# One exponential per wavelength, stacked sums, and a new order of VectorE's work in a multi-wavelength attention block

## The reference

```
for w in range(16):
    scores = einsum('bhqd,bhkd->bhqk', Q*m[w], K*m[w]) * SCALE      # m = cos(pm)
    scores = scores * cos(KERR * scores * scores)                    # KERR = 2.7e-12
    acc += softmax(scores) @ V * iw[w]
attn = (acc / 16) @ Wo + bo
x = layernorm(x + attn)
```

## Time and profile before

| what | value |
|---|---|
| three timed runs | 7163.84, 7164.55, 7164.82 us; median 7164.55 |
| the profiled execution's own time | 7165.78 us |
| its span, first to last instruction | 7164.2 us |
| TensorE's mean granted clock | 0.944 of full |
| ScalarE busy | 6960.6 us, 97% |
| TensorE busy | 5953.2 us, 83% |
| VectorE busy | 5710.1 us, 80% |

### The profile page before, as it was taken

How to read it: one execution, slowest core, us unless ns; L and a number is a source line. 1 busy time by engine, 2 the same in 40 slices (tenths; PEclk the granted TensorE clock), 3 DMA queues, 4 the chain that set the end, 5 groups by cost and what they waited for, 6 DMA issues and landing times.

```text
span 7164.2 us, 125922 instructions
## 1 busy us (share of the span) xinstructions
PE 5953.2 (83%) x46020; PEld 2131.5 (30%) x46020; DVE 5710.1 (80%) x7952; ACT 6960.6 (97%) x2227; POOL 116.6 (2%) x244
## 2 busy tenths in 40 slices
PE   7877878887888888888888888888888888888877
PEld 2222222222323233233233233233232332332335
DVE  6777877777888888888888888888888888888873
ACT  6999999999999999999999999999999999999992
POOL 0000000000000000000000000000000000000000
PEclk8999999999999999999999999999999999999998
DMA  2000000000001001001000010010010010010001
GB/s 61 2 4 4 4 2 4 4 2 17 23 21 29 17 27 29 18 25 32 20 27 29 15 29 23 22 29 23 24 32 17 27 29 16 27 29 18 27 19 36
DMA packets 61133, 151.59 MB, mean 21 GB/s; under 512 B 10272, under 2 KB 28576, under 8 KB 60320
## 3 DMA queue, kind: packets, MB, share of 16 engines
q1 hardware_dynamic: 55648, 140.04, 6.8%
q10 hardware_dynamic: 4160, 2.10, 0.1%
q0 software_dynamic: 768, 1.57, 0.1%
HBM read 132.66 MB, written 11.01 MB: 20 GB/s over the span
## 4 chain that ended last, share of the span: by engine, by line
ACT 56%; issue 25%; PE 10%; ACTq 7%; DVE 2%; DMA 0%; SPq 0%; DVEq 0%
ACT ring L592 55%; PE pv L661 6%; ACTq L587 5%; ACTq L588 1%; DVE scores L797 1%; PE sc L1120 1%; PE pv L668 1%; PE tr L1128 1%; PE sc L644 1%; ACT L606 0%; ACTq L580 0%; PE sc L625 0%; DVE rowmax L787 0%; PE sc L278 0%; ACTq L157 0%
## 5 line engine op out<-in xcount | busy, mean ns | idle before, releaser
L592 ACT ACTIVATE ring<-scores 128x4096 f32<-128x4096 f32 (+3 forms) x2048 | 6752.9, 3391 | 27.1 <-DVE scores L797 20.4
L661 PE MATMUL pv<-ring,vh 128*32 128x512 f32 x30720 | 4022.8, 638 | 1130.3 <-ACT ring L592 1123.0
L661 PEld LDWEIGHTS pv<-ring,vh 128*32 128x32 f32 x30720 | 1009.1, 115 | 3809.5 <-issue 2109.5
L829 DVE COPY numer<-pv 128x512 f32<-128x512 f32 x512 | 352.4, 688 | 481.6 <-PE pv L668 477.2
L797 DVE COPY scores<-sc 128x1024 f32<-128x1024 f32 (+1 forms) x512 | 601.9, 1217 | 75.7 <-PE sc L644 72.7
L823 DVE SCALAR_TENSOR_TENSOR vprobs<-ring,vprobs 128x1024 f32<-128x1024 f32 x512 | 627.2, 1225 | 19.1 <-issue 1.5
L822 DVE SCALAR_TENSOR_TENSOR vprobs<-vprobs,vbits 128x1024 f32<-128x1024 f32 x512 | 627.2, 1225 | 17.5
L787 DVE TENSOR_REDUCE rowmax<-sc 128x1 f32<-128x1024 f32 x512 | 601.4, 1216 | 40.2 <-PE sc L625 39.0
L821 DVE SCALAR_TENSOR_TENSOR vprobs<-ring 128x1024 f32<-128x1024 f32 x512 | 622.6, 1216 | 2.9
L668 PE MATMUL pv<-vpower,vlast 128*32 128x512 f32 x2048 | 532.1, 595 | 0.0
L668 PE MATMUL pv<-vprobs,vlast 128*32 128x512 f32 x2048 | 529.6, 592 | 0.0
(11 more groups left out here) (157 smaller groups left out, 2655.8 us busy)
## 6 DMA issues: line engine op xcount, KB each, us to landing
tile_w<-in_L_ffn_w SPq DMA_DIRECT2D x192, 512.0 KB, 4.0
qt<-q_scratch SPq DMA_DIRECT2D x256, 36.0 KB
kt_<-k_scratch SPq DMA_DIRECT2D x256, 36.0 KB
ring<-in_L_ffn_w SPq DMA_DIRECT2D x2, 2048.0 KB, 12.6
ring<-in_L_attn_x ACTq DMA_DIRECT2D x4, 512.0 KB, 7.4
q_scratch<-ring SPq DMA_DIRECT2D x4, 512.0 KB, 4.8
k_scratch<-ring SPq DMA_DIRECT2D x4, 512.0 KB, 5.6
v_scratch<-ring SPq DMA_DIRECT2D x4, 512.0 KB, 5.2
```

The lines of the kernel that those rows point to most:

```text
L592: nc.scalar.activation(ring[:, i % SLOTS, 0:cols], scores[:, bass.ds(n % 2, 1), half * CK:(half + 1) * CK, :].rearrange("p o k s -> p (o k ...
L661: last = nc.tensor.matmul(sums, vh[:, buf, half * CK + k, :], ring[:, 2 * half + w2, col:col + HALF], start=(half == 0 and k == 0), stop=( ...
```

## The change

- `ring` becomes 2 slots of 8192 columns. ScalarE makes all key tiles of a wavelength in one instruction, of 8192 columns for even wavelengths and 7168 for odd ones; the 1024 columns left out are VectorE's as before. It waits for the whole of the head's scores before the first, and loads its register before each.
- `weigh_values` takes one wavelength per step. The four column groups are now 2 query halves x 2 halves of the keys. Up to three wavelengths share a PSUM bank: the values stand in `vh` with zeros on both sides (`VW` columns), and a window of 32 columns moves by 9 for each of them, so that each adds into rows of its own. A bank is full after wavelengths 2, 5, 8, 11, 13 and 15 (`FILLS`).
- `copy_numer` copies one bank per fill, six per head in place of eight. `transpose_numer` is now four matmuls against a 64-column `fold` matrix, which add the two key halves and transpose at once; it runs behind the weighing in steps 3, 6, 9, 12 and 14, and the last one behind the weighing of step 0 of the next head. `normalise` runs three times per head in place of four (steps 6 and 12, and step 1 of the next head, followed there by `sum_wavelengths`).
- In `vector_head` the exponential work comes ahead of the maxima, the copies of scores and the tile's pieces of its step; `exponents` moves to odd steps and `polynomials` to even ones, for a pair that is used one step later than before. `exponents` gets a wait for the weighing that last read its `vpower` buffer.
- The tile's small matmuls of part 1 write to a bank of their own (`tr[:, 1]`) at separate columns and wait for `tile_logits_made` of the tile before instead of the normalisation; `tile_slice` 0 waits for `tile_x1T_made`.
- `layer_norm` takes three Newton steps in place of four.

The diff, cut to its core; of loops and functions that are rewritten only the new side is shown:

```diff
 G = 4
 QG = S // G
-NCH = 2 * W
 CK = KT // 2
-SLOTS = 4
+SLOTS = 2
+CHUNK = (KT * S, (KT - 1) * S)
+VR = D + 1
+STACK = 3
+VW = VC + (STACK - 1) * VR
+VAT = (STACK - 1) * VR
+FILLS = ((0, 1, 2), (3, 4, 5), (6, 7, 8), (9, 10, 11), (12, 13), (14, 15))
+NF = len(FILLS)
+FILL_OF = [f for f, ws in enumerate(FILLS) for _ in ws]
+GROUPED = [(f, f + 1) for f in range(0, NF, 2)]
 GT = 4
 NG = B * S // (GT * P)
...
-        ring = sb("ring", [P, SLOTS, CK * S])
-        vh = sb("vh", [P, 2, KT, VC])
+        ring = sb("ring", [P, SLOTS, KT * S])
+        vh = sb("vh", [P, 2, KT, VW])
-        vmant = ring[:, SLOTS - 1, (CK - 1) * S:CK * S]
-        vlast = sb("vlast", [P, 2, 2, VC])
+        vmant = ring[:, 1, CHUNK[1]:KT * S]
+        vlast = sb("vlast", [P, 2, 2, VW])
-        numer = sb("numer", [P, 2, HALF])
-        parts = sb("parts", [P, W // 2, 8, 2, D])
+        numer = sb("numer", [P, HALF])
+        parts = sb("parts", [P, 2 * KT, D, W // 2])
+        fold = sb("fold", [P, 2 * VC])
...
             then(nc.vector.tensor_scalar(y_.bitcast(I32), var_.bitcast(I32), -0.5, RSQRT_SEED, ALU.mult, ALU.add))
-            for _ in range(4):
+            for _ in range(3):
                 then(nc.vector.tensor_tensor(t_, y_, y_, ALU.mult))
                 then(nc.vector.scalar_tensor_tensor(t_, t_, -0.5, var_, ALU.mult, ALU.mult))
                 then(nc.vector.scalar_tensor_tensor(y_, t_, 1.5, y_, ALU.add, ALU.mult))
...
             def quads(n, first, last):
                 with act.Fori(first, last) as quad:
-                    for i in range(8):
-                        pair, half, w2 = i // 4, (i // 2) % 2, i % 2
-                        w, chunk = 4 * quad + 2 * pair + w2, NCH * n + 8 * quad + i
-                        if i in (0, 2):
-                            act.wait_ge(sc_free, USES * n + ROW_USE + 1 + CK * (half + 1))
-                        if half == 0:
-                            act.reg_load(scale[w2], scale_bits[:, bass.ds(w * H + n % H, 1)])
+                    for i in range(4):
+                        w, chunk = 4 * quad + i, W * n + 4 * quad + i
+                        if i == 0:
+                            act.wait_ge(sc_free, USES * (n + 1))
+                        act.reg_load(scale[i % 2], scale_bits[:, bass.ds(w * H + n % H, 1)])
                         act.wait_ge(slot_free, chunk + 1)
                         apart(act)
-
-                        cols = CK * S - (S if half == 1 and w2 == 1 else 0)
-                        nc.scalar.activation(ring[:, i % SLOTS, 0:cols],
-                                             scores[:, bass.ds(n % 2, 1), half * CK:(half + 1) * CK, :].rearrange("p o k s -> p (o k s)")[:, 0:cols],
-                                             ACT.Exp, scale=scale[w2]).then_inc(probs_ready, 1)
+                        nc.scalar.activation(ring[:, i % SLOTS, 0:CHUNK[i % 2]],
+                                             scores[:, bass.ds(n % 2, 1), :, :].rearrange("p o k s -> p (o k s)")[:, 0:CHUNK[i % 2]],
...
+        def weigh_values(pe, n, buf, w):
+
+
+            f = FILL_OF[w]
+            j, pair, w2 = FILLS[f].index(w), w // 2, w % 2
+            first, final = j == 0, w == FILLS[f][-1]
+            window = slice(VAT - j * VR, VAT - j * VR + VC)
+            if w == 0:
                 pe.wait_ge(vh_ready, n + 1)
+            pe.wait_ge(probs_ready, W * n + w + 1 + START)
             for k in range(CK):
                 for g in range(G):
+                    qh, kh = g // 2, g % 2
+                    kt = kh * CK + k
+                    sums, cols = pv[g * VC:(g + 1) * VC, f % 2, :], slice(qh * HALF, (qh + 1) * HALF)
+                    if kt == KT - 1 and w2 == 1:
+                        if qh == 0:
+                            pe.wait_ge(vexp_step, VSTEPS * (8 * n + pair) + POWER_STEP)
+                        nc.tensor.matmul(sums, vlast[:, buf, 0, window], vpower[:, pair % 2, cols], start=False, stop=final)
+                    else:
+                        last = nc.tensor.matmul(sums, vh[:, buf, kt, window], ring[:, w % SLOTS, kt * S + qh * HALF:kt * S + (qh + 1) * HALF],
+                                                start=(first and k == 0), stop=(final and k == CK - 1 and (kh == 1 or w2 == 0)))
+            if w2 == 1:
+                pe.wait_ge(vexp_step, VSTEPS * (8 * n + pair) + VSTEPS)
+                for qh in range(2):
+                    g = 2 * qh
+                    last = nc.tensor.matmul(pv[g * VC:(g + 1) * VC, f % 2, :], vlast[:, buf, 1, window],
+                                            vprobs[:, pair % 2, qh * HALF:(qh + 1) * HALF], start=False, stop=final)
+            last.then_inc(slot_free, 1)
+
+        def transpose_numer(pe, n, f):
+            if f % 2 == 0:
+                pe.wait_ge(tr_read, NF // 2 * n + f // 2 + START)
+            pe.wait_ge(pv_read, NF * n + f + 1)
+            for blk in range(4):
+                at = (f % 2) * 4 + blk
+                last = nc.tensor.matmul(tr[:, 0, at * 2 * VC:(at + 1) * 2 * VC], numer[:, blk * P:(blk + 1) * P],
+                                        fold[:, :], start=True, stop=True)
             last.then_inc(tr_full, 1)
...
+            for at in range(W):
+                weigh_values(pe, n, buf, at)
+                if at == 0:
+                    if carried:
+                        transpose_numer(pe, n - 1, NF - 1)
+                elif FILL_OF[at] != FILL_OF[at - 1]:
+                    transpose_numer(pe, n, FILL_OF[at - 1])
+                if more:
+                    if at == 0 and tile_no is not None:
+                        max_tile(pe, n + 1, 0, (tile_hidden_copied, 4 * tile_no + 3) if part == 2 else None)
+                        max_tile(pe, n + 1, 1, (tile_hidden_copied, 4 * tile_no + 4) if part == 2 else (tile_added, tile_no + START))
+                    elif at < 4:
+                        max_tile(pe, n + 1, 2 * at)
+                        max_tile(pe, n + 1, 2 * at + 1)
+                    elif at == 4:
+                        broadcast_rowmax(pe, n + 1)
+                    elif 6 <= at < 10:
+                        shifted_tile(pe, n + 1, 2 * (at - 6))
+                        shifted_tile(pe, n + 1, 2 * (at - 6) + 1)
...
-            bits, power = vbits[:, :], vpower[:, pair % 2, :]
-            then = stepper(dve, vexp_step, base, [0])
+            power = vpower[:, pair % 2, :]
             dve.wait_ge(sc_free, USES * (m + 1))
             if not first:
                 dve.wait_ge(vexp_step, base)
+                dve.wait_ge(slot_free, SLOTS + W * m + 2 * pair - 2)
             apart(dve)
 
-            then(nc.vector.tensor_scalar(bits, score, scales_log2[:, bass.ds((2 * pair + 1) * H + m % H, 1)], LOWEST, ALU.mult, ALU.max))
...
+        def copy_numer(dve, n, f):
+
+            dve.wait_ge(slot_free, SLOTS + W * n + FILLS[f][-1] + 1)
+            dve.wait_ge(tr_full, NF * n + f + START)
+            nc.vector.tensor_copy(numer[:, :], pv[:, f % 2, :]).then_inc(pv_read, 1)
+
+        def normalise(dve, n, g):
+
+            js = len(FILLS[GROUPED[g][0]])
+            dve.wait_ge(tr_full, NF * n + 2 * g + 2 + START)
+            blocks = tr[:, 0, :].rearrange("p (m r) -> p m r", r=VC)[:, :, 0:js * VR].rearrange("p m (j c) -> p m j c", c=VR)
+            nc.vector.reciprocal(recip[:, :, 0:js], blocks[:, :, :, D]).then_inc(norm_step, 1)
+            dve.wait_ge(norm_step, NF * n + 2 * g + 1)
+            nc.vector.tensor_tensor(coef[:, :, 0:js], recip[:, :, 0:js], wl_wide[:, g, :, :, 0:js].rearrange("p f t j -> p (f t) j"),
                                     ALU.mult).then_inc(norm_step, 1)
+            dve.wait_ge(norm_step, NF * n + 2 * g + 2)
+            nc.vector.tensor_tensor(parts[:, :, :, STACK * g:STACK * g + js].rearrange("p m d j -> p m j d"), blocks[:, :, :, 0:D],
+                                    coef[:, :, 0:js].rearrange("p m (j o) -> p m j o", o=1).to_broadcast([P, 2 * KT, js, D]),
                                     ALU.mult).then_inc(tr_read, 1)
         def sum_wavelengths(dve, n):
+            dve.wait_ge(tr_read, NF // 2 * (n + 1) + START)
             dve.wait_ge(att_stored, 32 * (n // H) + START)
+            nc.vector.tensor_reduce(att[:, :, bass.ds((n % H) * D, D)], parts[:, :, :, :].rearrange("p (f t) d x -> p (t d) f x", f=2),
                                     axis=AX.XY, op=ALU.add).then_inc(att_made, 1)
...
+        def vector_head(dve, n, i=None, part=0, then=None, more=True, carried=True):
+            for at in range(W):
+                if at == 1 and carried:
+                    normalise(dve, n - 1, NF // 2 - 1)
+                    sum_wavelengths(dve, n - 1)
+                if at in (6, 12):
+                    normalise(dve, n, at // 6 - 1)
+                if at + 1 == W or FILL_OF[at] != FILL_OF[at + 1]:
+                    copy_numer(dve, n, FILL_OF[at])
+                pair = (at + 3) // 2
+                step = exponents if at % 2 else polynomials
+                if pair < 8:
```

(28 more changed lines are left out.)

217 lines of the change are left out of this document (64 added, 153 removed).

## The result

The changed kernel takes **7081.06 us** (median of four timed runs, 7080.07 to 7081.89) against 7164.19 for the kernel before on the same chip. The interval of each ratio is wide beside the small differences, some 12 us to either side. Here the ratio is 0.9884, with an interval of 0.9867 to 0.9901: faster, inside the forecast's range (7040 to 7105) and 11 us above the forecast of 7070. The profiled execution took 7081.83 us, with a span of 7080.2 and a mean granted TensorE clock of 0.957 of full (0.944 before).

What follows compares the result with a forecast made beforehand. ScalarE was taken as the bound from its first exponential to its last. Span 7164.2 - 99.3 + 6.8 + 0.6 - 2.4 = 7069.9, forecast as 7070 us, 1.3% faster; range 7040 to 7105, chance 83%.

Steps and rivals of the forecast that it cites:

- ScalarE's instructions: On ScalarE's exponentials: 1024 fewer instructions at 0.097 us each give 99.3 us less; the columns stay the same.
- rival 1: On ScalarE's exponentials: each removed instruction gives back the whole 193 ns, 198 us in all, so 6971; chance 3%.
- the clock: TensorE's weighings at the lower clock level after idle gaps: none cost ScalarE anything, as 5.3 us fits in 6.07.
- part-1 chain: Token tile's work on TensorE, steps 12 to 15: could start at the lower level and lose its 2.0 us margin.
- Its own signs: In the profile: busy total near 6653 us, first start near 82.7; wrong if waits for weighings or scores exceed 25 us.
- The first head: Before ScalarE's first exponential: eight score tiles awaited instead of four, 6.8 us later, plus 0.6 for VectorE's setup.
- The tail: Last two groups: four layer norms on the path, each one Newton step shorter, 2.4 us less; closing work nothing.
- The ring: Two slots of a wavelength in place of four of half: same windows, 2.5 us per step left for other work.
- the tile chain: Part 1, steps 12 to 15, on TensorE: 30.0 us needed against 32.0 allowed, margin 2.0, so no cost.
- rival 2: Score tiles or fold matmuls overrun the 2.0 us margin by 0.8 in 48 heads: 38 us lost, about 7110; chance 8%.
- rival 3: Steps 0 to 9 of every head: TensorE at the lower clock becomes the bound, about 7220 with 64 pairs; chance 4%.
- VectorE's order: Steps 0 to 9 on VectorE: second score tile free 0.4 to 0.6 us before needed; cost nothing, bound 20 us.

Runs made afterwards that it cites:

- the two cuts: Each exponential of the changed kernel cut into two instructions, then into four, all else kept: 7171.57 us and 7366.86 us.
- the carry: Putting it back: the changed kernel with the last fold matmuls, normalisation and sum at the end of their own head: 7079.05 us, ratio 0.9882.

## Why the prediction was right, and where not

**ScalarE's instructions: right.** The sum said 99.3 us less; 95.4 came, of which the two cuts show 94.1 to be the instructions (1024 x 0.092). The 0.097 taken from starts was 5% high; the 193 ns that durations show (rival 1) would have been off by a factor of two. With it the prediction's reading holds that nothing else pays: with the instructions cut in two and all other parts kept, nothing of the gain is left, and putting back the carry, the order of VectorE or the Newton step changes the median by -2.0, -1.5 and +3.8 us, each within or near the scatter of the runs. (The lower end of the range was put down to an addition of 0.120; by the sum above it that gives 7046, not 7040.)

**The step that failed** is the last sentence of what the prediction said of the clock: none of the slow weighings cost ScalarE anything, "as 5.3 fits in 6.07". Three things were wrong in it. First, it took 5.34 us as the price of an even weighing at the lower level, but the granted clock over that row averages 0.68: part of it ran at the upper level. At the lower level four records follow the four before every 0.85 us where they do so every 0.43 at the upper, so a whole even weighing there would take about 7.0 us (an estimate, 3.64 + 8 x 0.42), and the one behind the GELU took 6.45. Neither fits in 6.07. Second, it looked at gaps of 1.27 and 2.52 us and not at the longest, behind the GELU, where TensorE waits 6.78 us. Third, its own had the cost already: the 5.1 us in 11 pieces are weighings in this very place. Stalls were summed at 0 more with a bound of 20; they were 10.5 more, within the bound but for 24 of 25 in another place than the one named for it (the second score tile of steps 3 and 7). The kernel with the old order and the matmuls in the gap shows the cause: the 15.6 us become 1.1. The Trainium skill ("TensorE: Matmul & The Clock Gate", section "HAM oscillation — how this bites in real kernels") has the rule that each burst behind such a gap starts at the slow clock. The trace agrees at this place, with a granted clock of 0.50 from the start of the weighing; a weighing behind 1.02 us of idle time took its full-speed 3.64. The prediction weighed that rule for the part-1 chain only, and in the head shown above that chain has no low weighing.

**Its own signs.** The busy total, 6657.5, and VectorE's wait before `exponents` (69.5 us for TensorE's weighings, none before) came as named. TensorE's wait for ScalarE is 869 us, a little under the 900 to 1000, and the first start is 81.15, before the 82.7. One sign of being wrong was badly set: waits of ScalarE "for scores" that "exceed 25 us". They are 27.2, but that is the 20.4 of the earlier trace rows plus the 6.8 that the prediction itself added.

**The first head.** Later by 5.9 us where 6.8 + 0.6 were summed. The copies came one pair after another, 3.4 us apart as before, but the first pair began at 67.71, 0.9 us earlier than the 68.59 of before, where 0.6 more had been summed for the setup. Why the setup became shorter wasn't traced.

**The tail.** 3.7 us in place of 2.4. Part is the last sum over wavelengths, within the 0.7 us that the prediction allowed for the closing work and left out: with the wavelengths innermost in memory it takes 1220 ns where it took 1952, 0.7 us less. VectorE's groups by shape after:

```profile
L861 DVE TENSOR_REDUCE att<-parts 128x1024 f32 x61 | 74.4, 1220 | 17.3 <-DVE parts L854 15.2
...
L854 DVE TENSOR_TENSOR parts<-tr,coef 128x256 f32<-128x256 f32 x64 | 40.6, 634 | 2.2
```

The product into `parts`, whose output is now strided, went the other way: 634 ns for 256 elements where it took 424, 0.2 us more. The rest wasn't traced to an instruction.

**The ring and the tile chain: right.** Two slots of a wavelength give the same windows as four of half; the chain took 29.6 us of 30.0 forecast and 32.0 allowed. Rivals 2 and 3 didn't come. The mechanism of rival 2 is real, though: the tripled fold matmuls show what it costs when a step's margin is gone. That of rival 3 came on a small scale, behind the GELU; its price per pair was too low, as it rests on the same 5.34.

**VectorE's order: right by luck.** "Free of VectorE 0.4 to 0.6 us before" was too hopeful; TensorE does wait, 35.3 us in 66 pieces. It cost nothing because the weighing has its 2.5 us, as the prediction said it would. But this holds only with three wavelengths to a bank, and only as long as no low stretch of the clock falls into these steps; stacking two (+41 us) and the matmuls in the gap (16.0 us of stalls in the new order, 1.1 in the old) show both.

**What stays open:** why the weighing behind the GELU varied from head to head in the kernel before and came out alike in all 24 heads of the changed one; why a gap of 0.91 us sits ahead of matmuls at the lower level in nine places of that run and not in the 15 others of its size, and why the matmuls behind the GELU made such gaps more frequent; what the carry and the order are worth in a kernel without the other parts, which wasn't tried; and what part of the tail's 3.7 us is left beside the Newton steps and the sum.

## What to carry to other kernels

When one engine bounds a kernel with a stream of equal instructions, the price of one more is read from starts that follow each other, not from durations: here 0.092 us against 0.19 shown. Cover on another engine is counted step by step, at the clock level that engine has behind its longest gap, because a burst that needs 3.6 us warm may need 6.5 just there. And parts that cost nothing one at a time can share the same margin: try them in pairs, and look at what the wait that "costs nothing" is standing on.

## What the runs showed of the hardware that was not expected

- A weighing of 16 matmuls took 6.45 us behind 6.78 us of idle time in the changed kernel, and 4.94 in one head and 6.54 in another behind the same 7.91 in the kernel before: the length of the gap alone doesn't set the loss; when the granted clock rises within the burst matters as much.
- Keeping TensorE busy with 22 useless matmuls in a gap is worth 13.7 us (7079.54 to 7065.84) with VectorE's old order and nothing with the new one (7081.06 to 7084.75).
- Each stall of ScalarE costs some 0.11 us beyond its own length, in lost overlap (7.03 against 6.92 us; 171 stalls more, 20.4 us more busy).
- The fold matmuls, 64 columns moving against 128x128, took 1.10 us for four, 0.27 each, against the 0.25 that the prediction took from the slice's 128 columns: half the columns made them no shorter.
